# Feed-forward norm sums: squares added in pairs on GpSimd, 12 products instead of 16, sums of values and squares in one column strip

## What is computed

```python
h = jnp.einsum('btd,hd->bth', x, absmean(W_fc))
h = jax.nn.gelu(h, approximate=False)
h = layernorm(h, ln_w, ln_b)
return jnp.einsum('bth,dh->btd', h, absmean(W_proj))
```

## Time and profile before

| what | value |
|---|---|
| median of 3 runs | 895.27 us (895.0 to 896.32) |
| the profiled execution | 892.54 us, of which its span is 890.9 us |
| TensorE busy | 815.3 us, 92% of the span |
| VectorE busy | 598.5 us, 67% |
| ScalarE busy | 488.7 us, 55% |
| GpSimd busy | 272.7 us, 31% |
| mean granted clock of TensorE | 0.977 of full speed |
| f32 sums of the norm (L974) | 256 records, 245.6 to about 402 us |

### The profile page before, as it was taken

The page is one execution under the profiler, slowest core; times in us unless marked ns, Lnnn a source line. Parts: engine busy times, 40 slices in busy tenths (PEclk is TensorE's granted clock), DMA queues, the critical chain, the costliest instruction groups (busy, mean ns, idle before and its releaser), DMA issues. The chain is left out here.

```text
span 890.9 us, 23450 instructions
## 1 busy us (share of the span) xinstructions
PE 815.3 (92%) x8950; PEld 667.5 (75%) x8950; DVE 598.5 (67%) x1439; ACT 488.7 (55%) x1018; POOL 272.7 (31%) x335
## 2 busy tenths in 40 slices
PE   6999999998899999998999899998988879999960
PEld 5888888887677777766777688886655549999950
DVE  3677778778557777778555425577667886657627
ACT  2544443443777777775974244556575435454426
POOL 1257763221112222224000000124443134656344
PEclk9999999999999999999999999999999989999985
DMA  8600000000000000001478534435222314566439
GB/s 321 197 21 22 18 24 18 18 12 3 1 1 1 1 1 1 1 1 34 126 196 199 132 92 131 136 101 198 93 85 99 103 31 121 142 201 161 119 64 343
DMA packets 74637, 79.55 MB, mean 89 GB/s; under 512 B 21824, under 2 KB 65728, under 8 KB 74176
## 3 DMA queue, kind: packets, MB, share of 16 engines
q1 hardware_dynamic: 69584, 72.36, 26.6%
q0 software_dynamic: 3968, 5.25, 3.4%
q10 hardware_dynamic: 1008, 0.91, 0.3%
HBM read 50.70 MB, written 27.79 MB: 88 GB/s over the span
## 5 line engine op out<-in xcount | busy, mean ns | idle before, releaser
L729 DVE TENSOR_TENSOR r_prob<-r_pS,const 128x512 f32<-128x512 f32 x128 | 81.9, 682 | 24.7 <-PE r_pS L551 24.7
L1106 DVE SCALAR_TENSOR_TENSOR f_gl<-att_res,small_first,f_gh 128x512 fp32r<-128x512 f32 x64 | 47.3, 747 | 35.7 <-ACT f_gh L1031 33.4
L1685 POOL TENSOR_TENSOR att_res<-att_res,t_hy 128x1024 f32<-128x1024 f32 x8 | 15.5, 1958 | 165.2 <-DVEq L2182 165.2
L960 PE MATMUL f_pY<-wpjT,f_gh 128*128 128x256 f32 x256 | 65.4, 290 | 0.3 <-DVE f_gl L1106 0.3
L961 PE MATMUL f_pY<-wpjT,f_gl 128*128 128x256 f32 x256 | 62.7, 279 | 0.0
L1374 PEld LDWEIGHTS q_bank<-q_xT,att_res 128*64 128x64 f32 x1024 | 57.3, 140 | 7.2 <-issue 4.2
L1374 PE MATMUL q_bank<-q_xT,att_res 128*64 128x128 f32 x1024 | 60.9, 279 | 0.0
L960 PEld LDWEIGHTS f_pY<-wpjT,f_gh 128*128 128x128 f32 x256 | 48.1, 188 | 15.9 <-issue 13.4
L2595 POOL DMA_INDIRECT sum_dram<-e_yo,y_id x24 | 43.1, 1795 | 54.6 <-ACT e_yo L2732 39.5
L1025 ACT ACTIVATE att_res<-f_pH 128x512 f32<-128x512 f32 x64 | 38.0, 594 | 38.6 <-PE f_pH L945 37.8
L2713 ACT ACTIVATE e_hh<-e_pH 128x320 fp32r<-128x320 f32 x64 | 26.2, 433 | 54.0 <-PE e_pH L2637 53.8
(11 more groups left out here) (336 smaller groups left out, 2350.6 us busy)
## 6 DMA issues: line engine op xcount, KB each, us to landing
kv_dram<-att_res SPq DMA_DIRECT2D x32, 256.0 KB, 3.5
t_ring<-kv_dram SPq DMA_DIRECT2D x128, 64.0 KB, 2.3
wi<-L_ffn_wi SPq DMA_DIRECT2D x8, 1024.0 KB, 5.0
wo<-L_ffn_wo SPq DMA_DIRECT2D x8, 1024.0 KB, 7.6
x_res<-L_attn_x SPq DMA_DIRECT2D x8, 512.0 KB, 7.0
q_dram<-att_res SPq DMA_DIRECT2D x16, 256.0 KB, 3.5
t_q<-q_dram SPq DMA_DIRECT2D x8, 512.0 KB, 4.4
x_dram<-x_res SPq DMA_DIRECT2D x8, 512.0 KB, 3.0
```

The lines of the kernel that those rows point to most:

```text
L729: dve.tensor_tensor(prob[t % 2][:, r, :, :], pS[r][:, :, :], dec[:, r, :, :], ALU.mult)\
L960: pe.matmul(out, gh[c % 4][:, cols], net.wpjT[:, c, :], start=(c == 0 and t % 2 == 0), stop=False, skip_group_check=True)
L1106: dve.scalar_tensor_tensor(out=gl[c % 4][:, :], in0=g[c][:, :], scalar=net.lnw[:, c:c + 1], in1=gh[c % 4][:, :], op0=ALU.mult, op1=ALU.sub ...
```

## The change

GpSimd now adds the squares of each two neighbouring chunks in place (`pair`: `gg[c] += gg[c+1]` for c = 0, 2, 4, 6), so a batch has 8 products of values and 4 of squares. A half makes 6 products, dealt to the strips in turn, going on where the first half stopped. Each strip holds sums of values in its rows 0 to 15 and sums of squares in rows 16 to 31: the weights are two new constants, `ones_low` and `ones_high`, with ones in 16 of 32 columns. The second half moves from chunk 1 to chunk 2 of the next batch, the copy from 2 to 3, the gathering and the moments from 3 to 4. On GpSimd the additions stand in the loop, with the reciprocal root of the batch before between the second and the third of them. The sums wait for GpSimd's additions and GELU instead of the squares, and for the variance instead of the copy of the gathered sums.

```diff
-    parts["sums"] = np.stack([(p // 32 % 2 == k) / (32.0 * HID) for k in range(2)], 1)
+    parts["sums"] = np.stack([(p // 16 % 2 == k) / (16.0 * HID) for k in range(2)], 1)
+    for k, name in enumerate(("ones_low", "ones_high")):
+        parts[name] = np.tile(np.arange(32) // 16 == k, (P, 1)).astype(np.float64)
...
-            pe.wait_ge(squared.sem, squared.after(NH * b + 4 * q + 4))
+            pe.wait_ge(gelued.sem, gelued.after(NH * b + 4 * q + 4))
+            pe.wait_ge(paired.sem, paired.after(4 * b + 2 * q + 2))
             if q == 0:
-                pe.wait_ge(sums_taken.sem, sums_taken.after(b))
+                pe.wait_ge(var_ready.sem, var_ready.after(b))
...
-            for c in (4 * q, 4 * q + 2):
-                for s in range(4):
-                    part = (g, gg)[s % 2][c + s // 2]
-                    mm = pe.matmul(pS[32 * s:32 * s + 32, :], net.table["ones"][:, 0:32], part[:, :], start=(c == 0), stop=(c == NH - 2))
+            plain = [(net.table["ones_low"], g[c]) for c in range(4 * q, 4 * q + 4)]
+            squares = [(net.table["ones_high"], gg[c]) for c in (4 * q, 4 * q + 2)]
+            for n, (which, part) in enumerate(plain + squares, 6 * q):
+                s = n % 4
+                mm = pe.matmul(pS[32 * s:32 * s + 32, :], which, part[:, :], start=(n < 4), stop=(n >= 8))
...
-                if b and c == 1:
+                if b and c == 2:
                     sum_strips(b - 1, 1)
-                if b and c == 3:
+                if b and c == 4:
                     gather_sums(b - 1)
...
         def square(b, c):
+            act.wait_ge(summed.sem, summed.after(2 * b + c // 4 - 1))
...
-                if b and c == 2:
+                if b and c == 3:
                     keep_sums(b - 1)
...
-        for b in range(BATCH):
-            inner(b)
-            if b == BATCH - 1:
-                mean_squares(b - 1)
-            outer(b)
-            if b != BATCH - 2:
-                mean_squares(b)
+        def pair(b, c):
+            pool.wait_ge(squared.sem, squared.after(NH * b + c + 2))
+            pool.tensor_tensor(gg[c][:, :], gg[c][:, :], gg[c + 1][:, :], ALU.add).then_inc(paired.sem, 1)
+
+        for b in range(BATCH + 1):
+            for c in range(0, NH, 2):
+                if b < BATCH:
+                    pair(b, c)
+                if b and c == 2:
+                    inner(b - 1)
+                    if b == BATCH:
+                        mean_squares(b - 2)
+            if b:
+                outer(b - 1)
+                if b != BATCH - 1:
+                    mean_squares(b - 1)
...
-                if b and c == 3:
+                if b and c == 4:
                     moments(b - 1)
```

More of the change, by code:

```diff
@@ L92, in constant_table @@
     return np.concatenate([a for a in parts.values()], 1).astype(np.float32), where
-LAYER0_CONSTS = ("block", "qdecay", "kdecay", "tiledecay", "even", "odd", "decay")
+LAYER0_CONSTS = ("block", "qdecay", "kdecay", "tiledecay", "even", "odd", "ones_low", "ones_high", "decay")
 CONSTS, WHERE = constant_table(LAYER0_CONSTS, False)
@@ L914, in ternary_ffn @@
     turned, xh_ready, xl_ready = (ph.sig(n) for n in ("turned", "xh_ready", "xl_ready"))
-    up_made, gelued, high, split, squared = ph.sig("up_made"), ph.sig("gelued", 2), ph.sig("high"), ph.sig("split", NH), ph.sig("squared")
+    up_made, gelued, high, split, squared, paired = ph.sig("up_made"), ph.sig("gelued", 2), ph.sig("high"), ph.sig("split", NH), ph.sig("squared"), ph.sig("paired")
     down_made, y_taken = ph.sig("down_made", 4), ph.sig("y_taken", 2 * TPB)
-    summed, sums_kept, sums_made, sums_taken = ph.sig("summed", 2), ph.sig("sums_kept"), ph.sig("sums_made"), ph.sig("sums_taken")
+    summed, sums_kept, sums_made = ph.sig("summed", 2), ph.sig("sums_kept"), ph.sig("sums_made")
     var_ready, rs_ready, rows_ready, yrs_ready = (ph.sig(n) for n in ("var_ready", "rs_ready", "rows_ready", "yrs_ready"))
@@ L920, in ternary_ffn @@
     step, pool_step = ph.sig("step"), ph.sig("pool_step")
-    net.y_taken, net.gelued, net.sums_taken, net.q_rs_ready, net.x_ready = y_taken, gelued, sums_taken, q_rs_ready, ph.sig("x_ready")
+    net.y_taken, net.gelued, net.sums_taken, net.q_rs_ready, net.x_ready = y_taken, gelued, var_ready, q_rs_ready, ph.sig("x_ready")
     def tensor(pe, last_of_retention, inputs):
@@ L1121, in moments @@
                 dve.wait_ge(rs_ready.sem, rs_ready.after(b))
-            dve.tensor_copy(both[:, :, :], pB).then_inc(sums_taken.sem, 1)
-            dve.wait_ge(sums_taken.sem, sums_taken.after(b + 1))
+            dve.tensor_copy(both[:, :, :], pB).then_inc(steps.sem, 1)
+            dve.wait_ge(steps.sem, steps.done(1))
             dve.tensor_tensor(var[:, :], both[:, :, 0], both[:, :, 0], ALU.mult).then_inc(steps.sem, 1)
```

## The result

The changed kernel takes 903.79 us in the median of 4 runs (902.02 to 904.91), the kernel before 895.13 (894.42 to 896.32). The ratio is 1.0094, with a 95% interval of 1.0073 to 1.0114: 0.9% slower. The profiled execution took 902.02 us, with a span of 900.3.

The account below looks back on a forecast made before the run. TensorE was taken to set the pace, busy 21.85 of 22 us. Terms 0 + 3.9 + 1.6 + 3.0 + 0.5 = 9.0 us on the median of 895.27 gave 904.3 us, range 897.0 to 910.0.

Parts of the forecast that it names:

- 12 products for nothing: Sums on TensorE: 6 products a half still take two rounds, 1.86 us as before, so 0 gained.
- a price for each product: Rival at the sums: emptier rounds are shorter, giving back 7.4 us, to 896.9 us; chance 0.12.
- The wait in batch 0: TensorE's first sums wait for two GpSimd additions, which start only after retention: 3.9 us, bounds 2.8 and 4.6.
- the higher of my two figures: First sums of batch 0: 4.2 us late instead of 3.6 if a VectorE low-part correction gets in between.
- The clock: Behind batch 0's wait, TensorE's clock falls once to half speed for 3.4 us: 1.6 us lost, bounds 0 and 1.7.
- The wait ahead of gathering: TensorE waits 0.65 us instead of 0.22 for ScalarE's copy in 7 batches: 3.0 us, bounds 0 and 3.0.
- The last batch: Last down-projection and turning of inputs go ahead of the last sums, moments come later: 0.5 us, bounds 0 and 1.0.
- down until about 401.0, turning until 401.9: Last batch on TensorE: the turning directly follows the last down-projection, with the sums running from 402.0 to 403.8.
- VectorE late as well: Rival: additions hold back VectorE's two-SBUF-operand work until TensorE waits in 7 batches, 5.6 us more, 909.9 us; chance 0.2.

Follow-up runs that it names:

- run 1: Changed kernel with two more products in each half of the sums, in the strips its second round leaves empty: 905.37 us, ratio 1.0118 to the kernel before.
- run 2: Changed kernel with the same 12 products dealt 8 and 4 to the halves instead of 6 and 6: 897.19 us, ratio 1.0032 to the kernel before.
- run 3: Changed kernel without additions ahead of the first half of batch 0, which takes 8 products: 898.15 us, ratio 1.0032 to the kernel before.
- run 4: Changed kernel with ScalarE's copy of the strips ahead of GELU of chunk 3 instead of behind its square: 907.84 us, ratio 1.0143 to the kernel before.
- run 10: Changed kernel with only the last sums put ahead of the turning of the next stage's inputs: 902.92 us, ratio 1.0099 to the kernel before.
- run 5: Kernel before with only the moved steps (second half, copy, gathering, moments one chunk later), 16 products, no additions: 901.13 us, ratio 1.0057.
- run 6: Kernel before plus the 32 GpSimd additions, written into a tile nothing reads; first sums wait for the variance: 900.14 us, ratio 1.0055.
- run 11: The kernel of run 8 with the copy of the strips also put ahead of GELU of chunk 3: 901.15 us, ratio 1.0072 to the kernel before.
- run 7: Kernel before with the moved steps and the copy of the strips ahead of GELU of chunk 3, no additions: 894.71 us, ratio 0.9995.
- run 8: Changed kernel, products dealt 8 and 4 (batches 1 to 7), no additions ahead of batch 0's first half, last sums before turning: 891.01 us, ratio 0.9949 to before.
- run 9: Kernel before with one edit, the copy of the strips ahead of GELU of chunk 2 instead of behind its square: 892.15 us, ratio 0.9966.

## Why the prediction was right

The time lies 0.5 us from the forecast of 904.3, and part of that is luck. The terms as the traces measure them add up to 4.24 + 1.7 + 2.3 + 2.25 = 10.5 us, not 9.0, while the medians differ by 8.7. In the profiles the books close: 10.5, and 0.5 that the changed one was late before, less 1.7 for a fall of the clock that the kernel before has at 416.5 and the changed one hasn't, make the 9.3 at the third turning. The four costs came where and why they were forecast, but for a wait in the last batch that made that term much too small. One by one:

- **12 products for nothing** was right: 1.84 us a half. Runs 1 and 2 show it from both sides, the first with more products at the same time, the second with the same products in fewer rounds. The rival of a price for each product falls with them.
- **The wait in batch 0** was right in place and cause (run 3). I took 3.9 us and it was 4.24. The addition was priced at 1.13 us, between two rows of other shapes, and takes 1.26 at the least and 1.34 in the median. Of the two that count, the first took 1.26 and the second 1.71, beside a low part of VectorE from 247.65 to 249.19: the collision that the higher of my two figures allowed for.
- **The clock** fell as expected and cost 1.7 us. All five traces with this wait of 4.2 us (the changed kernel, runs 1, 2, 4 and 10) have a fall behind it. The fall at 416.5 is another matter: it comes and goes from one execution to the next, as the last section shows, and its absence is no effect of the change.
- **The wait ahead of gathering** was right in size, and its count was wrong. I took 3.0 us for 7 batches. The last of the seven has no turning at chunk 2, so it had waited 0.58 us before already (the row below); six batches with 0.4 make 2.4, and the stretch from the clock's return to the last batch shows 2.3 (8.74 less 4.78 and 1.7).

```profile
387.12 1.05 PE L981 MATMUL f_pS<-const,f_strips 128*128 128x2 f32 x8 [0.58 <-ACT f_strips L1040]
```

- **The last batch** was mis-sized: 0.5 us forecast, 2.25 measured (10.99 less 8.74). The step that failed is "down until about 401.0, turning until 401.9". I let the turning follow the down-projection at once. It has to wait until VectorE has taken the rows of the batch before out of the bank (f_y), 1.37 us. Before, the sums stood ahead of it and covered this wait: the last of these rows was taken at 402.46, and the turning began at 403.18. Run 5 shows the same 1.37 us without any addition. What is left of the 2.25 are the 0.37 us for a low part and the 0.70 for the copy, less the 0.61 that the sums waited before, and 0.4 that no wait in the list names.

```profile
401.98 0.48 DVE L1141 SCALAR_TENSOR_TENSOR f_y<-f_pY,f_rs,f_xb 128x256 f32<-128x256 f32 x1
...
403.18 1.04 PE L1363 MATMUL q_bank<-const,q_xn 128*128 128x128 f32 x8
```


- **VectorE late as well** didn't happen in the changed kernel: its steady batches have no new wait for a low part, and the 0.37 us in the last batch stand in run 5 as well (402.73), without additions. Its price was real all the same. The variance step of four columns took 1.06 us where an addition held it up, against 0.16, and run 6 loses 2.9 us in the batches to the additions alone. In the changed kernel such delays lie under the wait for the copy, which gives VectorE 0.4 us more a batch. Runs 4 and 11 take that cover away, and run 7 takes the additions away as well, and with them the waits.

What stays open: whether falls of the clock account for the 1.8 us by which the medians differ less than the terms add up to. How much of run 6 is VectorE held up and how much the late root. And the 0.54 us that the changed kernel's profile was late before its first sum: the five traces without the new constants begin this stage's first turning at 223.96 to 224.49, the eight with them at 224.23 to 225.25. These overlap, so it may be scatter or the larger table; it wasn't tried by itself.

## What to carry to other kernels

Products in column strips cost by rounds, as far as these runs go (f32, 512 columns, four strips of 32): count the largest number that falls to one strip in a group, not the products, and deal them so that no round is left half empty. A copy that another engine waits for belongs where its own engine is idle, ahead of the work that it doesn't need; look at what the engine was waiting for just before. The gain comes only if no other delay lies under the wait that goes: the same move gained 3 us in the kernel before and lost 4 and 10 us where the additions held VectorE up. Work given to GpSimd can be counted as free only where VectorE isn't running operations with two SBUF operands beside it and where GpSimd's program has reached it: its first use stands behind all that comes before.

## What the runs showed of the hardware

A VectorE operation with two SBUF operands that meets a GpSimd addition isn't slowed in proportion, it can be held until that ends. The timeline of the changed kernel shows both engines: first VectorE's step on four columns, then GpSimd's addition in its way.

```profile
314.23 1.06 DVE L1139 TENSOR_TENSOR f_var<-f_both 128x4 f32<-128x4 f32 x1
...
313.94 1.33 POOL L1093 TENSOR_TENSOR f_gg<-f_gg 128x512 f32<-128x512 f32 x1 [3.31 <-ACT f_gg L1040]
```

VectorE's low part and the addition in the list of tiles, over all occurrences (ns min/median/max, from when to when):

```profile
L1121 DVE SCALAR_TENSOR_TENSOR f_gl<-att_res,small_first,f_gh x64: 730/750/1673, 233.4 to 408.0; 128x512 fp32r<-128x512 f32 x64
...
L1093 POOL TENSOR_TENSOR f_gg<-f_gg x32: 1257/1335/1772, 247.4 to 409.0; 128x512 f32<-128x512 f32 x32
```

The step ends at 315.29, the addition at 315.27. The additions have their long cases too (1.77 us against 1.26), such as the second one of batch 0. The Trainium skill ("SBUF — State Buffer", section "Who interferes with whom") has one rule for this, an exclusive lock on the shared ports; this trace agrees.

The clock is the other. Ahead of the second turning TensorE stands idle for 2.1 us in six of the thirteen kernels of this document and for 2.62 in seven. A fall followed in four of the six (the kernel before, runs 6, 10, 11; not in 8 and 9) and in four of the seven (runs 2, 3, 5, 7; not in the changed kernel, 1 and 4). So neither the kernel nor the length of these two waits decides it, and only the wait of 4.2 us had a fall behind it every time. A fall in this part of the program took about 3.4 us and 1.7 us of work each time. That puts a scatter of a microsecond or two on any comparison of single executions of this kernel.
